# One PSUM pair for four time tiles: VectorE's two tiles ahead of ScalarE's, where each engine had a bank of its own

## The reference, cut to what matters

```python
dt = softplus(dt @ W_dt + b_dt)
dA = exp(dt[..., None] * A)                      # decay, per channel, state and token
dBu = (dt * xc)[..., None] * Bm[:, :, None, :]
h = associative_scan over tokens of (a1 * a2, a2 * b1 + b2) on (dA, dBu)
y = einsum('blds,bls->bld', h, Cm) + D_skip * xc # sum over the 16 states
y = y * silu(z)
x + y @ W_out
```

## Time and profile before

| what | value |
| --- | --- |
| median of three runs | 1801.06 us |
| the profiled execution | 1802.19 us, of it a span of 1799.4 us |
| busy: TensorE, VectorE, ScalarE, GpSimd | 75%, 75%, 50%, 56% of the span |
| costliest: GpSimd L483, VectorE L1086, ScalarE L652, TensorE L861 | 639.5, 608.4, 347.5, 328.3 us |

### The profile page before, as it was taken

The page is one execution under the profiler, slowest core; times in us unless marked ns, Lnnn a source line. Parts: engine busy times, 40 slices in busy tenths (PEclk is TensorE's granted clock), DMA queues, the critical chain, the costliest instruction groups (busy, mean ns, idle before and its releaser), DMA issues. The chain is left out here.

```text
span 1799.4 us, 27604 instructions
## 1 busy us (share of the span) xinstructions
PE 1349.5 (75%) x7872; PEld 1096.3 (61%) x7873; DVE 1342.3 (75%) x2523; ACT 897.4 (50%) x1322; POOL 1012.5 (56%) x848
## 2 busy tenths in 40 slices
PE   4566666667667677677677675547899999999994
PEld 1344544545555455554554464437799999999994
DVE  4889989989788998998997999464455555555552
ACT  3767667667567567667657565222122222222220
POOL 2676867867767768768758777211233333333331
PEclk8889889888788898898898988756999999999997
DMA  6311111311310410410400401144723222322224
GB/s 211 101 47 48 42 36 41 114 41 35 115 40 15 141 36 19 141 36 19 122 26 19 123 32 39 48 153 130 228 48 57 53 53 53 57 57 53 53 53 114
DMA packets 88774, 128.03 MB, mean 71 GB/s; under 512 B 12816, under 2 KB 62608, under 8 KB 88416
## 3 DMA queue, kind: packets, MB, share of 16 engines
q1 hardware_dynamic: 70176, 93.09, 16.8%
q0 software_dynamic: 16128, 28.39, 8.4%
q10 hardware_dynamic: 2368, 5.36, 0.9%
HBM read 100.13 MB, written 30.88 MB: 73 GB/s over the span
## 5 line engine op out<-in xcount | busy, mean ns | idle before, releaser
L483 POOL TENSOR_TENSOR dBu<-u,brep 128x512 f32<-128x512 f32 x512 | 639.5, 1289 | 141.0 <-DVE hs L1086 64.2
L1086 DVE TENSOR_TENSOR_SCAN hs<-psum,dBu 128x512 f32<-128x512 f32 x512 | 608.4, 1207 | 62.1 <-ACT psum L652 53.9
L861 PE MATMUL psum<-ident,hs 128*128 128x128 f32 x2048 | 328.3, 312 | 204.2 <-DVE y L1097 155.7
L652 ACT ACTIVATE psum<-dt,aneg 128x512 f32<-128x512 f32 x512 | 347.5, 688 | 227.1 <-DVE hs L1086 223.4
L861 PEld LDWEIGHTS psum<-ident,hs 128*128 128x128 f32 x2048 | 265.7, 160 | 290.5 <-DVE y L1097 204.3
L1546 ACT ACTIVATE w_now<-w_sb 128x2048 f32 x72 | 137.5, 1911 | 395.8 <-PE psum L1568 378.3
L1528 POOL DMA_INDIRECT sum_d<-ysb,row_of_sum x72 | 114.3, 1587 | 339.1 <-DVE ysb L1634 336.2
L1568 PE MATMUL psum<-xgT,w_now 128*128 128x128 f32 x2304 | 273.4, 278 | 0.0
L870 PE MATMUL psum<-ident,hc 128*128 128x128 f32 x1024 | 187.0, 316 | 113.9 <-ACT hc L636 75.0
L1568 PEld LDWEIGHTS psum<-xgT,w_now 128*128 128x128 f32 x2304 | 267.5, 195 | 0.1
L1579 PE MATMUL psum<-w_sb,hT 128*128 x1152 | 260.4, 379 | 0.0
(11 more groups left out here) (193 smaller groups left out, 1372.1 us busy)
## 6 DMA issues: line engine op xcount, KB each, us to landing
brep<-b_d SPq DMA_DIRECT2D x128, 256.0 KB, 3.2
w_sb<-in_W SPq DMA_DIRECT2D x16, 1024.0 KB, 5.4
h_d<-hmod SPq DMA_DIRECT2D x8, 512.0 KB, 3.0
modo<-mod_d SPq DMA_DIRECT2D x8, 512.0 KB, 5.9
xres<-in_x SPq DMA_DIRECT2D x8, 512.0 KB, 6.9
hres<-h_d SPq DMA_DIRECT2D x8, 512.0 KB, 7.7
xhat_d<-modo SPq DMA_DIRECT2D x8, 512.0 KB, 3.8
xhat_d<-hres SPq DMA_DIRECT2D x8, 512.0 KB, 5.9
```

The source lines that it names most:

```text
L483: nc.gpsimd.tensor_tensor(dBu[:, i % RING, :], u[:, p, c, :], brep[:, s % 4, :], ALU.mult).then_inc(s_dBu, 1)
L652: nc.scalar.activation(dA[:, i % DA_RING, :], dt[:, p, c, :], ACT.Exp, scale=aneg[:, c, s:s + 1]).then_inc(s_dA, 1)
L861: last = nc.tensor.transpose(T[:, i // DT, c * P:(c + 1) * P], hs[:, s % 2, c, i * P:(i + 1) * P], ident[:, :])
L1086: nc.vector.tensor_tensor_scan(hs[:, s % 2, c, :], dA[:, i % DA_RING, :], dBu[:, i % RING, :], 0.0, ALU.mult, ALU.add).then_inc(s_scan, 1)
```

## The change

The two banks take the tiles in turn: tile i goes into bank i % 2. TensorE transposes in the order 0, 1, other work, 2, 3, so VectorE's tiles come first and ScalarE's follow in the same banks. Tile 0 now waits for ScalarE's read of tile 2 of the state before, tile 1 for its read of tile 3, tile 2 for VectorE's read of tile 0, tile 3 for that of tile 1. VectorE reads tile 1 after the second scan, not after the third. ScalarE makes decays 0 and 1, does the middle work, makes decays 2 and 3, then `times_c` 0 and 1, then the end work.

```diff
@@ times_c (ScalarE)
-                act.wait_ge(s_tr, n * UNITS + TI * s + 2 * k + 2)
+                act.wait_ge(s_tr, n * UNITS + TI * s + DT + k + 1)
                 after(act, s_acc, 2 * (n * NS + s) + k - 1)
-                nc.scalar.activation(hc[:, k, :], T[:, 1, :], ACT.Copy, scale=ct[:, p, DT + k, s:s + 1]).then_inc(s_hc, 1)
+                nc.scalar.activation(hc[:, k, :], T[:, k, :], ACT.Copy, scale=ct[:, p, DT + k, s:s + 1]).then_inc(s_hc, 1)
@@ body of ScalarE
                     decays(n, p, s, (0, 1), has_o)
-                    times_c_before(n, p, s, 0, has_o)
-                    decays(n, p, s, (2,), has_o)
...
-                    decays(n, p, s, (3,), has_o)
+                    decays(n, p, s, (2, 3), has_o)
+                    times_c_before(n, p, s, 0, has_o)
                     times_c_before(n, p, s, 1, has_o)
@@ states (TensorE)
                 if i < DT:
-                    after(pe, s_y, DT * (n * NS + s) + i)
+                    after(pe, s_hc, 2 * (n * NS + s) + i - 1)
                 else:
-                    after(pe, s_hc, 2 * (n * NS + s) + i - DT)
+                    pe.wait_ge(s_y, DT * (n * NS + s) + i - DT + 1)
                 for c in range(CH):
-                    last = nc.tensor.transpose(T[:, i // DT, c * P:(c + 1) * P], hs[:, s % 2, c, i * P:(i + 1) * P], ident[:, :])
+                    last = nc.tensor.transpose(T[:, i % 2, c * P:(c + 1) * P], hs[:, s % 2, c, i * P:(i + 1) * P], ident[:, :])
@@ body of TensorE
                     states(n, s, 0)
-                    states(n, s, 2)
+                    states(n, s, 1)
...
-                    states(n, s, 1)
+                    states(n, s, 2)
                     states(n, s, 3)
@@ add_y (VectorE)
-                dve.wait_ge(s_tr, n * UNITS + TI * s + 2 * i + 1)
+                dve.wait_ge(s_tr, n * UNITS + TI * s + i + 1)
...
-                    ins = nc.vector.scalar_tensor_tensor(y[:, i, :], T[:, 0, :], c_s, y[:, i, :], ALU.mult, ALU.add)
+                    ins = nc.vector.scalar_tensor_tensor(y[:, i, :], T[:, i, :], c_s, y[:, i, :], ALU.mult, ALU.add)
@@ body of VectorE
                     next_scan(s, 1)
+                    add_y(n, p, s, 1)
                     next_scan(s, 2)
-                    add_y(n, p, s, 1)
                     next_scan(s, 3)
```

More of the change, by code:

```diff
@@ L1093, in add_y @@
                     after(dve, s_yT, n)
-                    ins = nc.vector.tensor_scalar(y[:, i, :], T[:, 0, :], c_s, None, ALU.mult)
+                    ins = nc.vector.tensor_scalar(y[:, i, :], T[:, i, :], c_s, None, ALU.mult)
                 else:
                     dve.wait_ge(s_y, DT * (n * NS + s - 1) + i + 1)
-                    ins = nc.vector.scalar_tensor_tensor(y[:, i, :], T[:, 0, :], c_s, y[:, i, :], ALU.mult, ALU.add)
+                    ins = nc.vector.scalar_tensor_tensor(y[:, i, :], T[:, i, :], c_s, y[:, i, :], ALU.mult, ALU.add)
                 ins.then_inc(s_y, 1)
```

## The result

The changed kernel took 1813.3 us (median of 4 runs, 1811.8 to 1815.9) against 1800.7 us before (four runs, among them the three of the 1801.06 above): 1.0071 times the time, with a 95% interval of 1.0055 to 1.0087. It is 12.6 us slower. The forecast was 5 us faster, and 1813 lies outside its range, 2 us above the upper end. The profiled execution has a span of 1814.0 us, 14.6 more than before.

A forecast was written before the change was run, and what follows sets the result against it. VectorE sets the pace, with 104 us idle in the sequences. Minus 0.65 us a sequence gave minus 4 for six middle ones; with 0 and minus 1 for sequences 0 and 7, minus 5 from 1802.2: 1797 us, range 1783 to 1811.

The forecast's parts named there:

- none of the four: Lower clock in the four bare steps besides 6 and 14: 3.6 us a sequence, 29 in all, left out.
- Rival 1: Chain tile 1, tile 3, times_c 1, decay 0 becomes the bound in bare steps; slower, 1811 or 1804 us; chance 0.25.
- Step 6, minus 3.9: ScalarE's silu block starts earlier, so VectorE's 4.26 us wait goes; minus 3.9 us a middle sequence.
- the rule weighed in the prediction: Silu block: a 1.38 us drain with every table load, 2.66 per switch; would give plus 4 us; not used.
- Step 7, 0: x_proj: both times_cs stand behind it, then xd_copy holds the decay; 0, taken without the full clock.
- Step 9, plus 0.9: o_xhat at ScalarE's end (2.06 us): 0.9 us showed before, 1.8 after; plus 0.9 us a sequence.
- step 10, minus 0.55: The 0.49 us wait for tile 1 behind dt_proj goes, with 0.07 of overlap; minus 0.55 us a sequence.
- Step 0, plus 0.7: TensorE's y_t stands behind add_up 1 of step 15, so the next sequence's tile 0 is late; plus 0.7 us.
- Step 1, plus 0.75: norm_t (1.26 us): 1.1 us show, where some 0.3 did before; plus 0.75 us a sequence.
- step 14, plus 1.1: norm (1.69 us): 0.93 before; after, 1.6 and 0.45 for a transpose at the lower clock; plus 1.1 us.
- The chain of 2.9 us: Tile 1, transpose, times_c 1, decay 0: exactly as long as VectorE's own three pieces; the open price.
- The signs: Profile after: no step 6 scan wait over 1 us, tile waits 33 to under 20 us, decay waits 50 to 60.

The follow-up runs named there:

- e5: Changed kernel with TensorE's transposes of tile 1 made three times and of tile 2 twice, in step 8 alone; 1798.9 us.
- e1: Kernel before with ScalarE's two silus and their table loads in step 7 ahead of decay 2, not behind it; 1774.4 us.
- e3: Changed kernel with ballast in steps 6, 8, 14 and 15: transposes of tile 1 made three times, of tile 2 twice; 1781.0 us.
- e6: Changed kernel with y_t behind tile 3 in step 15, ahead of add_up 0, and norm in ScalarE's middle of step 15; 1789.0 us.
- e11: Changed kernel with VectorE reading tile 1 before the second scan, and ScalarE's order decay 2, times_c 0, times_c 1, decay 3; 1812.9 us.
- e4: Changed kernel with ScalarE's times_c 0 between decays 2 and 3; 1802.9 us.
- e7: Kernel before: silus early, x_proj halved, xd_copy in step 9's middle, c_t behind add_up 0 of step 8, norm in step 15's middle; 1765.5 us.
- e9: e7 with squares ending step 9, o_xhat ending step 11, step 0's two add_ups behind step 1's first two tiles; 1743.6 us.

## Why the prediction was wrong

**The failed step is the price of steps 9 and 10: the clock there was taken as full, and TensorE's queue was not followed to the scores.** The prediction wrote of the lower clock: "I take it for none of the four, as nearest to the plain stretch at 1.00". Rival 1 had the lower clock, but not the place: it priced transposes in the bare steps, and most of the loss is the wait for the scores and for tile 0 behind them. That its 1811 us is 2 us from the result is luck; I gave it 0.25. Against it I counted the mean clock of the kernel before, which tells nothing about an order that cuts TensorE's work differently. The decisive figure is that of the stretch itself: 0.67 in place of 1.00. It nearly doubled everything in one long chain: transposes, scores (3.42 for 1.85 us), `dt_proj` (2.07 for 1.12), sum, transposes. With ballast in step 8 alone (e5) steps 9 and 10 come out at plus 0.8 and minus 0.3 us against the kernel before, near the plus 0.9 and minus 0.55 of the sum, and the time is 1 us below the kernel before, where the forecast was 5: 14 of the 18 us of error hang on this one stretch.

Term by term:

- **Step 6, minus 3.9:** measured minus 4.05, and e1 confirmed it from the other side (1774 expected, 1774.4 measured). The table load took 1.28 us again, the silu began 1.30 after its start, and of the drain in the rule weighed in the prediction nothing showed.
- **Step 7, 0:** measured minus 0.9. `x_proj` ran at the full clock (3.6 us, not 4.4); the prediction had put that case at minus 1.1 and did not take it.
- **Step 9, plus 0.9, step 10, minus 0.55:** measured plus 2.2 and plus 0.2, the largest miss, 2.1 us a sequence, more than the whole error of a middle sequence (2.0). I priced only ScalarE's tail there. ScalarE's queue was followed to its end, but TensorE's second piece of other work was not: it now waits for hc of tile 2, behind both decays. At the full clock that alone is 0.88 us of wait (e3), about the size of the tail it runs beside, so that the 0.9 came out near by luck; at half the clock it is 3.1 and then 2.6. The wait of 0.49 us that was to go in step 10 was also no mean: in the six middle sequences it is 0.15 to 0.49 in four and absent in two.
- **Step 0, plus 0.7:** measured plus 1.5. The mechanism held (e6 took it back), but eight transposes of `y_t` and the next ones ran at the lower clock; with e3's ballast step 0 is 1.2 us shorter.
- **Step 1, plus 0.75, and step 14, plus 1.1:** measured plus 0.9 and plus 0.8.
- **Steps 2 to 5, plus 0.35:** nothing was lost. **Step 15, 0:** plus 0.4.
- **The chain of 2.9 us** is not what bounds the changed kernel: of the steps without other work on VectorE, 6 is 6.1 and 15 is 6.4 us long, against 5.8 by the replay. e11, which loosened it, gained nothing, but delayed decays instead, so how tight the chain is was not measured by itself.
- **The parts outside the middle sequences:** 0 and minus 1 were predicted; 1.8 us for sequence 0 and some 5 for the last one and what follows were measured. I did not take these apart.
- **The signs:** the silu wait went and the waits ahead of scans stayed at 50 to 60 us in all (58.8), mostly where they were expected. But the waits for tiles rose to 38 us and did not fall under 20, and the clock over the sequences, 0.82, is just at the bound that the prediction had named for rival 1.

What stays open: how much the ballast of steps 6, 14 and 15 gives each, what ballast would give the kernel before, why the clock ahead of the scores is 0.67 in four of the middle sequences and 0.84 in two with much the same work, and how much of e4's 10 us is order and how much is clock.

## What to carry to other kernels

- An order that cuts one engine's work into smaller groups with pauses between them can lower TensorE's clock, as it did here from 1.00 to 0.67, and then each late piece behind it costs nearly twice. It shows in the time only where the order has left that chain no room (e7). Read the granted clock of the very stretch where the order changes, not a mean, and price the chain behind it at both levels.
- Replay every engine's queue through the moved wait, the second piece of other work too. Of a change with many parts, run the one part that gains by itself: here it was worth 26 us, and what was added to it cost 39.
- A wait of the pacing engine over 0.9 us was mostly other work in the wrong place of some queue; moving seven such pieces brought 31 us on top (e1 to e9). They were moved in groups of four and three, so what each is worth was not measured, and one step (10) grew by 1.75 us.

## What the runs showed of the hardware that was not expected

**More matmuls, less time.** Twelve repeated transposes in each of four steps (e3) made the kernel 32 us faster and TensorE's busy time in the sequences 18 us shorter (807 to 789).

**Short instructions of VectorE are long beside GpSimd's.** In `o_top` of the kernel before, while GpSimd multiplied:

```profile
709.79 3.72 POOL L483 TENSOR_TENSOR dBu<-u,brep 128x512 f32<-128x512 f32 x3
709.84 1.25 DVE L1139 TENSOR_TENSOR vd<-top 128x4 f32<-128x4 f32 x1
711.01 1.31 DVE L1141 CAST tif<-tix 128x8 f32<-128x8 uint32 x1
712.46 1.20 DVE L1143 TENSOR_TENSOR oh<-iota,tif 128x32 f32 x2
```

and in the changed kernel, where VectorE came later and GpSimd's last multiplication began at 718.82:

```profile
718.82 1.26 POOL L483 TENSOR_TENSOR dBu<-u,brep 128x512 f32<-128x512 f32 x1
719.53 0.57 DVE L1138 TENSOR_TENSOR vd<-top 128x4 f32<-128x4 f32 x1
720.03 0.16 DVE L1140 CAST tif<-tix 128x8 f32<-128x8 uint32 x1
720.33 0.32 DVE L1142 TENSOR_TENSOR oh<-iota,tif 128x32 f32 x2
```

The same CAST of 8 elements takes 1.31 or 0.16 us. In the first rows the three multiplications follow each other every 1.24 us and end at about 711.0, 712.3 and 713.5, the VectorE instructions at 711.1, 712.3 and 713.7; in the second both end at 720.1. So a VectorE instruction ended about when the GpSimd instruction beside it did. The Trainium skill ("SBUF — State Buffer", Terms) has it that the two engines share a port pair that one of them holds for its whole instruction while the other blocks; the rows agree with that. Three such lines of `o_top` account for most of the 19 us by which VectorE's busy time fell: `oh` 11.2 to 2.2 us, CAST 6.9 to 1.1, `vd` 8.6 to 5.9 in all. It also hid part of the loss: step 10 has 3.5 us of waits in the changed kernel (2.62 for tile 0 and 0.83 for the decay ahead of the next scan) and 0 to 0.5 before, and is only 0.2 us longer. No run tried it by itself, so the cause is only argued.
